# Decoder layer on one core: the half-swapped q and k go back into the projection's PSUM bank, and the projection units get fixed banks

## The reference

```python
q, k, v = x @ Wq + bq, x @ Wk + bk, x @ Wv + bv        # 16 heads of 32
q, k = rope(q), rope(k)        # x * cos + swapped_pairs(x) * sin
attn = softmax(causal(q @ k.T / sqrt(32)));  x = layernorm(x + (attn @ v) @ Wo + bo)
x = layernorm(x + x @ softmax(query(ctx) @ key(ctx).T))     # cross attention, ctx (4, 512, 256)
x = layernorm(x + (silu(x @ Wg.T) * (x @ Wu.T)) @ Wd.T)     # 512 -> 2048 -> 512
```

## Time and profile before

| | |
|---|---|
| time, median of 3 runs (lowest, highest) | 1027.92 us (1027.11, 1029.76) |
| time of the profiled execution | 1029.37 us |
| its span, first to last instruction | 1027.6 us |
| mean granted TensorE clock | 0.988 of full |
| PE, DVE, ACT, POOL busy in the span | 977.9, 628.3, 494.0, 352.0 us |

### The profile page before, as it was taken

The page is one execution under the profiler, slowest core; times in us unless marked ns, Lnnn a source line. Parts: engine busy times, 40 slices in busy tenths (PEclk is TensorE's granted clock), DMA queues, the critical chain, the costliest instruction groups (busy, mean ns, idle before and its releaser), DMA issues.

```text
span 1027.6 us, 15734 instructions
## 1 busy us (share of the span) xinstructions
PE 977.9 (95%) x5416; PEld 792.2 (77%) x5416; DVE 628.3 (61%) x1341; ACT 494.0 (48%) x1078; POOL 352.0 (34%) x356
## 2 busy tenths in 40 slices
PE   7879999999998889899999999999999999999997
PEld 5657777777776667688888888888888888888886
DVE  5677787778874787655544475454476444564434
ACT  5576766777774674344432344332444422333332
POOL 2566646655864523222112141111141121131112
PEclk9998999999999999899999999999999999999999
DMA  5976666955765661262221244221244212243201
GB/s 219 245 184 157 172 180 157 247 138 145 217 165 133 185 172 55 93 227 75 88 93 62 92 164 164 71 84 63 92 169 159 92 63 77 83 178 113 93 31 42
DMA packets 45486, 134.53 MB, mean 131 GB/s; under 512 B 5472, under 2 KB 5600, under 8 KB 42720
## 3 DMA queue, kind: packets, MB, share of 16 engines
q1 hardware_dynamic: 45408, 133.52, 42.5%
HBM read 104.14 MB, written 25.17 MB: 126 GB/s over the span
## 4 chain that ended last, share of the span: by engine, by line
PE 79%; POOL 6%; DVE 5%; issue 4%; ACT 4%; DMA 2%; SPq 0%; DVEq 0%; POOLq 0%; ACTq 0%
PE pu L588 17%; PE pg L588 17%; PE pd L588 17%; PE pj L536 10%; PE pj L588 5%; PE pv L579 4%; PE ps L551 2%; ACT prob L758 2%; PE pa L564 2%; PE pb L564 2%; PE pj L594 2%; POOL raw L1194 1%; DVE prob L961 1%; POOL raw L1199 1%; POOL raw L1203 1%
## 5 line engine op out<-in xcount | busy, mean ns | idle before, releaser
L1284 POOL TENSOR_TENSOR g_lo<-gated,g_hi 128x512 fp32r<-128x512 f32 x63 | 81.3, 1290 | 429.3 <-ACT g_hi L849 429.3
L758 ACT ACTIVATE prob<-prob,nmax 128x512 f32<-128x512 f32 (+3 forms) x256 | 143.8, 562 | 109.5 <-DVE nmax L961 109.2
L961 DVE CUSTOM_DVE_ANT_0 prob<-ps,mask 128x512 f32<-128x512 f32 (+3 forms) x256 | 122.6, 484 | 80.2 <-PE ps L551 76.8
L1071 DVE TENSOR_TENSOR dn_lo<-f_raw,dn_hi 128x512 fp32r<-128x512 f32 x63 | 51.2, 812 | 114.3 <-ACT dn_hi L833 114.3
L551 PE MATMUL ps<-ks,qs 128*128 128x256 f32 (+2 forms) x256 | 106.3, 417 | 11.2 <-DVE nmax L961 8.2
L1092 DVE SCALAR_TENSOR_TENSOR half<-th,pg 128x512 f32<-128x512 f32 x63 | 43.2, 686 | 100.5 <-ACT th L840 100.5
L588 PE MATMUL pd<-dn_hi,g_hi 128*128 128x512 f32 x252 | 100.0, 397 | 0.0
L840 ACT ACTIVATE th<-pg 128x512 f32<-128x512 f32 x63 | 37.7, 598 | 127.6 <-PE pg L588 127.6
L588 PE MATMUL pd<-dn_lo,g_hi 128*128 128x512 f32 x252 | 98.4, 390 | 0.0
L588 PE MATMUL pd<-dn_hi,g_lo 128*128 128x512 f32 x252 | 98.1, 389 | 0.0
L849 ACT CAST g_hi<-gated 128x512 fp32r<-128x512 f32 x63 | 39.1, 621 | 118.8 <-DVE gated L1099 118.8
(11 more groups left out here) (198 smaller groups left out, 2237.6 us busy)
## 6 DMA issues: line engine op xcount, KB each, us to landing
f_raw<-in_w_ffn SPq DMA_DIRECT2D x64, 768.0 KB, 4.3
qs<-qk_scratch SPq DMA_DIRECT2D x64, 256.0 KB, 4.7
ks<-qk_scratch SPq DMA_DIRECT2D x60, 256.0 KB, 7.7
qk_scratch<-qk_hi SPq DMA_DIRECT2D x32, 256.0 KB, 2.0
qk_scratch<-raw SPq DMA_DIRECT2D x32, 256.0 KB, 2.0
res<-in_x SPq DMA_DIRECT2D x4, 1024.0 KB, 4.9
x_scratch<-res SPq DMA_DIRECT2D x4, 1024.0 KB, 5.4
x<-x_scratch SPq DMA_DIRECT2D x4, 1024.0 KB, 4.8
```

The source lines that it names most:

```text
L758: act.activation(prob[:, t % PROBS, 0:w], prob[:, t % PROBS, 0:w], ACT.Exp, bias=nmax[:, n % 2, i:i + 1], scale=-1.0, accum_out=rsum[:, n ...
L961: dve.tensor_tensor_reduce(prob[:, t % PROBS, 0:w], ps[:, t % 2, 0:w], mask[:, S - w:S], -D ** -0.5, 3e38, ALU.add, ALU.min, accum_out=nma ...
L1071: dve.tensor_tensor(lo, f_raw[i % NR][:, 2 * KT * P:], hi.bitcast(F32), ALU.subtract).then_inc(dnlo_done, 1)
L1284: pool.tensor_tensor(lo, gated[:], hi.bitcast(F32), ALU.subtract).then_inc(glo_done, 1)
```

## The change

Three edits belong together. (1) For all groups but the first, `swap` writes its result not to `swp` but back into the PSUM bank from which the projection came, and `times_sin` reads it there and writes `swp`. The wait that `swp` be free again (`rot_done`) moves from `swap` to `times_sin`. (2) The bank is thus occupied until the sine product is done: `emptied` waits for `sin_done` where it waited for `raw_done`. (3) The banks are fixed by kind: q in bank 0, k and r in bank 1, the v or o unit that starts in slot 11 in bank 0, the one that starts in slot 15 in bank 1; and each k unit but the first starts one slot later. `LAST` is rewritten for the same.

```diff
-LAST = [(("q", 14), 195, (3, 3, 3, 3), 0), (("r", 11), 199, (4,), 1), (("k", 14), 200, (4, 4, 4), 0),
-        (("q", 15), 203, (3, 3, 3, 3), 1), (("o", 8), 203, (3, 3, 3, 3), 2), (("c", 0), 206, (6,), 0),
-        (("k", 15), 208, (4, 4, 4), 1), (("o", 9), 208, (4, 4, 4), 2), (("c", 1), 209, (6,), 0),
+LAST = [(("q", 14), 195, (3, 3, 3, 3), 0), (("r", 11), 199, (4,), 1), (("k", 14), 201, (4, 4, 4), 1),
+        (("q", 15), 203, (3, 3, 3, 3), 0), (("o", 8), 203, (3, 3, 3, 3), 2), (("c", 0), 207, (6,), 1),
+        (("k", 15), 209, (4, 4, 4), 1), (("o", 9), 208, (4, 4, 4), 2), (("c", 1), 209, (6,), 0),
...
+def pj_bank(key, start):
+    return {"q": 0, "k": 1, "r": 1, "b": 0}.get(key[0], start % TILES // 12)
...
-        out.append((("k", n), TILES * n - 24, (4, 4, 4)))
+        out.append((("k", n), TILES * n - (23 if n else 24), (4, 4, 4)))
...
-    return [unit + (n % 2,) for n, unit in enumerate(out)] + LAST
+    return [unit + (pj_bank(unit[0], unit[1]),) for unit in out] + LAST
...
     def emptied(eng, key):
         kind, n = key
+        if kind in "qk" and n:
+            eng.wait_ge(sin_done, 2 * n + "qk".index(kind) + 1)
+            return
...
         def swap(n, u):
             dve.wait_ge(raw_done[u], n + 1)
-            if n or u:
-                dve.wait_ge(rot_done, 2 * n + u)
-            dve.stream_shuffle(swp[:], raw[:, u, :], SWAP).then_inc(swap_done, 1)
+            if n == 0 and u:
+                dve.wait_ge(rot_done, 1)
+            dve.stream_shuffle(over[PLACE["qk"[u], n][0]] if n else swp[:], raw[:, u, :], SWAP).then_inc(swap_done, 1)
 
         def times_sin(n, u):
+            if n:
+                dve.wait_ge(rot_done, 2 * n + u)
             dve.wait_ge(swap_done, 2 * n + u + 1)
-            dve.tensor_tensor(swp[:], swp[:], sin[:], ALU.mult).then_inc(sin_done, 1)
+            dve.tensor_tensor(swp[:], over[PLACE["qk"[u], n][0]] if n else swp[:], sin[:], ALU.mult).then_inc(sin_done, 1)
```

More of the change, by code:

```diff
@@ L942, in swap, with times_sin @@
             dve.wait_ge(raw_done[u], n + 1)
-            if n or u:
+            if n == 0 and u:
+                dve.wait_ge(rot_done, 1)
+            dve.stream_shuffle(over[PLACE["qk"[u], n][0]] if n else swp[:], raw[:, u, :], SWAP).then_inc(swap_done, 1)
+        def times_sin(n, u):
+            if n:
                 dve.wait_ge(rot_done, 2 * n + u)
-            dve.stream_shuffle(swp[:], raw[:, u, :], SWAP).then_inc(swap_done, 1)
-        def times_sin(n, u):
             dve.wait_ge(swap_done, 2 * n + u + 1)
-            dve.tensor_tensor(swp[:], swp[:], sin[:], ALU.mult).then_inc(sin_done, 1)
+            dve.tensor_tensor(swp[:], over[PLACE["qk"[u], n][0]] if n else swp[:], sin[:], ALU.mult).then_inc(sin_done, 1)
         def row_max(t):
```

## The result

The changed kernel takes **1047.2 us** in the median of 4 runs (1043.8 to 1049.17), beside 1027.51 us (1025.59 to 1029.76) for the kernel before in the same session: ratio 1.0187, 95% interval 1.0153 to 1.0222. It is slower by 19.7 us. The forecast was 1039.7, range 1033 to 1049: the direction and the mechanism are right, and the loss is 8 us larger than its sum of +11.8.

The account below looks back on a forecast made before the run. The prediction took PE's own instructions to bound groups 3 to 11. Its terms, 17.0 + 0.7 - 1.4 - 1.2 - 2.1 - 1.2 = +11.8 us, on the median of 1027.92 gave 1039.7, range 1033 to 1049.

Parts of the forecast that it names:

- Stall of 2.07 per group: In each group, PE's first matmul of k waits for ACT's copy of r, losing 2.07 us.
- Relief of 0.37 per group: At each group's end, PE's waits of 0.21 and 0.16 go; net cost 1.70 us per group.
- rival (b): In each of ten groups the clock falls in the stall: +12 us more, 1052; chance 0.05.
- Groups 12 and 13: The stall of k14 falls into PE's wait for `c_lo`, which is ready at the same time: -1.2 us.
- Group 0 and its fall of the clock: In group 0, three waits behind maxima shrink, -1.4 us, and the first clock fall goes, -1.2 us.
- Groups 1 and 2: Group 1's delay falls mostly into existing waits, +0.7 us; group 2 pays the stall, +1.70, and loses its clock fall, -2.1.
- Rival (c): In eleven groups the swap into PSUM takes twice as long, 0.74 us more each: +8 us, 1048; chance 0.07.
- (a): PE reaches k as late as ACT's copy of r, so the wait costs nothing: 1018 us; chance 0.07.
- (d): Half the stall, 1.0 us per group, is absorbed by unseen relief: loss 7, 1031 us or less; chance 0.07.

Follow-up runs that it names:

- experiment 3: The kernel before, with POOL's cosine product waiting for the sine product from group 1 on, nothing in PSUM: 1024.72 us, ratio 0.9965.
- experiment 2: The changed kernel with the swapped halves in SBUF again, its order of PE and fixed banks kept: 1047.96 us, ratio 1.0193.
- experiment 1: The changed kernel with ACT's copy of r one slot earlier, ahead of the exponential of slot 8: 1022.29 us, ratio 0.9936.
- experiment 4: The changed kernel run once more, unchanged, for a second trace: 1043.02 us, a single execution.
- Experiment 7: The changed kernel with the copy of r one slot earlier, weights of o 13 slots later, context loads two slots earlier: 1016.55 us, ratio 0.9889.
- experiment 12: The changed kernel with the copy of r ahead of slot 7's exponential, weights of o later, context loads earlier: 1010.07 us, ratio 0.9821.
- experiment 10: The kernel before with k one slot later, not in r's bank, cosine behind sine, weights of o later, context loads earlier: 1017.16 us, ratio 0.9893.
- experiment 5: The kernel before with k one slot later from group 1 on, in a bank not shared with r: 1024.70 us, ratio 0.9966.

## Why the prediction was right in sign and too small in size

**What a wait of PE costs.** One line fits five kernels: an undisturbed group is 21.05 us, plus for each wait the idle time shown plus 0.27 (both numbers taken from two of them, the other three follow). What it leaves of the sixth comes with the falls of the clock.

| kernel | waits shown | 21.05 + shown + 0.27 each | measured |
|---|---|---|---|
| before, group 5 | 0.21, 0.16 | 21.96 | 22.01 |
| changed | 1.91 | 23.23 | 23.24 |
| copy one slot earlier | 0.23 | 21.55 | 21.55 |
| k later in its own bank | 0.16 | 21.48 | 21.47 |
| copy ahead of the exponential | none | 21.05 | 21.06 |
| copy one slot later | 3.37 | 24.69 | 27.27, so 2.6 with the clock |

The 0.27 can be read in the timeline: a matmul is shown 0.39 long, but the next starts 0.235 later, so 0.16 of the wait is hidden under the shown end; and the first matmul after a wait is followed after 0.33 instead of 0.235. The shortest idle time that the profile lists is 0.15, so small ones can hide: groups 5 and 9 of experiment 3 take 21.4 with none listed.

**Step by step.**

- *Stall of 2.07 per group: right.* By the line above it is 1.91 + 0.27 = 2.18. Place, count (12, and one in group 13) and length (1.9) are as forecast.
- *Relief of 0.37 per group: the term of the steady groups that was mis-sized.* Two waits shown as 0.21 and 0.16 cost 0.91. The net loss of an undisturbed group is 2.18 - 0.91 = 1.27; measured 1.25 (21.98 to 23.23), where 1.70 was forecast. In groups 6 and 10 the relief is larger still, some 2.0: a third wait of 0.9 goes too, and the net loss is 0.14. I had read the waits off group 5 alone. The reason given for the relief was half right: experiment 2 shows that in most of these groups the pause brings it and the shorter sine adds nothing; in groups 5 and 9 the sine adds 0.5.
- *"The clock falls in each stall", rival (b) with a chance of 0.05: partly true.* It fell behind four stalls of nine at 1.55 us each, 6.2 us. That I set it against single waits of 1.04 and 1.41 over which the clock stayed up was too weak a ground. Groups 3 to 11 came out at +15.1 against 15.3 forecast, and that is luck: seven groups at 1.24, two at 0.14 and four falls at 1.55 make 15.2, so the relief that was too small and the falls that were left out cancel.
- *Groups 12 and 13, -1.2 forecast, +3.1 measured: the largest miss of this trace.* The stall of k14 did vanish in the wait for `c_lo`: group 12 grew by 0.5 only (30.24 to 30.73), and takes 30.68 without that stall (experiment 1). But `c_lo` was not ready "at the same time": it ended 27.4 us into its group (349.40 less 321.97) instead of 26.4 (330.20 less 303.78), and ahead of it ACT had waited 2.33 for the context's transfers, where it had waited 0.37. I had seen these transfers coming a slot later and had set that off against POOL's cosine of k. In the repetition (experiment 4) the set-off holds: ACT waits 0.50, `c_lo` ends at 26.4 again (344.56 less 318.15), and group 12 takes 28.37, 1.9 less than before, as forecast. So this half of the miss is one execution's. Experiment 7, with these loads two slots earlier, shortened the group by 5.2. Group 13 grew in both, by 2.57 and 2.39: k15 waits 1.31 for ACT's move of c0, which shares its bank (forecast 0.7), and the first product behind it 2.33 for POOL's `cqk_lo` instead of 1.1 (not in my sum at all). Other waits went in return: all that are listed in the group sum to 5.7 us, 5.2 before. Some 1.6 of the 2.57, by the price of a fall above, comes with a fall of the clock right behind the 2.33 (mean 0.95 in this group, 1.00 before), which the sum doesn't have either. Timeline of ACT, POOL and PE there:

```profile
340.79 0.62 ACT L792 CAST p_hi<-p_raw 128x512 fp32r<-128x512 f32 x1 [2.33 <-DMA pbias<-in_bctx]
...
347.05 2.35 POOL L1264 TENSOR_TENSOR c_lo<-c_raw,c_hi 128x1024 fp32r<-128x1024 f32 x1
...
349.54 0.76 PE L544 MATMUL pj<-c_hi,p_hi 128*128 128x512 f32 x1 [2.47 <-POOL c_lo L1264]
355.91 0.50 PE L544 MATMUL pj<-xT_hi,w_hi 128*128 128x512 f32 x1 [1.31 <-ACT c_raw L798]
368.98 0.47 PE L544 MATMUL pj<-cqk_hi 128*128 128x512 f32 x1 [2.33 <-POOL cqk_lo L1270]
```

- *Group 0 and its fall of the clock, -1.4 and -1.2 forecast, -0.1 measured.* PE ran the first slots at full clock and then stood, because ACT's move of the next q waits for a store (ACT, PE, then the windows around the stall and behind it):

```profile
44.47 0.69 ACT L756 ACTIVATE raw<-pj,bcol 128x512 f32<-128x512 f32 x1 [3.38 <-DMA qk_scratch<-raw]
...
46.54 0.58 PE L559 MATMUL ps<-ks,qs 128*128 128x256 f32 x1 [3.29 <-DVE nmax L971]
...
40.00:46.50 6.50, 3.25 (x20) 2.38 (x18) 2.82 (x11) 2.27 (x8) 0.53 (x1) 0.90 0.86 283
46.50:53.30 6.80, 6.76 (x20) 4.94 (x21) 2.73 (x10) 5.55 (x13) 5.68 (x5) 0.59 1.06 214
```

  The move starts at 44.47, where before it was at 44.38: the store's landing is the bound. The gain became idle time, and the clock fell during this stall, and for longer, instead of at the group's start. With the weights of o out of the way (experiment 7) group 0 takes 22.15.

- *Groups 1 and 2: +0.7 and -0.4 forecast (+1.70 for the stall, -2.1 for the clock), +2.06 and +1.08 measured.* In group 1 the stall did fall into the other waits in good part: they sum to 3.7 us instead of 4.7. What is above the forecast is a fall of the clock (0.93); in the repetition, with the clock at 1.00, the group takes 22.10, no more than the 22.15 of before. In group 2 the long fall that I took away was replaced by a shorter one (0.93 instead of 0.82), and beside the stall PE waits 1.99 for ACT's copy of the transposed probabilities, where its three waits were 1.05 in all; no experiment looked into that wait.
- *Rival (c), a slow swap into PSUM: false*, 0.690 us. *Rivals (a) and (d)*: the copy did not come in time; relief beyond mine was 0.5 in seven groups of nine, not 1.0.

The sum of the misses, against the forecast of each: group 0 +2.5, group 1 +1.4, group 2 +1.5, groups 3 to 11 -0.2, groups 12 and 13 +4.3; the rest, cross attention and feed-forward, ran 1.4 us shorter in the span of after (in code that is the same, which no experiment looked into). Together 8 us: the spans differ by 19.8. The late transfer in group 12 and the falls of the clock in groups 1 and 13 are some 5 of it. For the repetition the spans differ by 13.6 only, 1.8 more than the sum.

**What stays open.** Why a stall of 1.91 us lowers the clock in some groups and not in others, and one of 3.38 not in group 1, is not settled. Nor is it shown whether the late weights of o or the shorter groups make the load of `ks` late in group 1 (3.10 and 3.40 us of waiting in experiments 12 and 10).

## What to carry to other kernels

When an edit puts two units into one buffer, look up who empties the buffer and what stands ahead of it in that engine's program: here 0.57 us of copying behind an exponential cost 2.2 us per group on the engine that bounds the kernel, and moving that one copy ahead turned a loss of 1.9% into a gain of 1.0%. Judge a part of a bundle by itself: the PSUM operand was worth some 0.4%, the later slot 0.3%, and the shared bank cost 2.3% (experiments 5 and 2), more than all the rest gives. Work taken from an engine that does not set the time is worth only the waits of the engine that does, and a pause elsewhere takes these away as well. And take a second trace before explaining single stretches: two executions of the changed kernel differ by 6.2 us, 4.5 of it in two groups out of sixteen.

## What the runs showed of the hardware

- The stream shuffle of 128x512 fp32 took 0.690 us into PSUM and 0.742 into SBUF; the product with one PSUM operand 0.685, with both in SBUF and POOL idle 0.692. The 62 cycles that the Trainium skill, page "VectorE: DVE Perf Modes", section "The TRN2 errata", charges for a PSUM source do not show in these, where one operand is in PSUM and one in SBUF.
- The idle time shown ahead of a matmul is too short by 0.27 us here. With many small waits that is more than the waits: two of 0.37 in all cost 0.91.
- The clock's reaction to one stall per group went from no group of nine (0.23 us) over four (1.91) to all (3.37), and a fall cost 1.55 us at 1.91 and 2.6 at 3.37. It makes the price of a wait of PE grow faster than the wait: the last 1.46 us cost 4.0. The falls lasted 3.4 us at 1.91 and 6.8 at 3.37.
